# One tile's hat to GpSimd and one tile's distances to VectorE in bump attention, with a new order of all engines' work

## The chip, the core and the metric

The kernel runs on one core of a Trainium2 chip, in one launch. The metric is the device time in microseconds. Its engines are TensorE (matrix products), VectorE, ScalarE and GpSimd (elementwise work), and SyncE, which only issues transfers here. Each takes its instructions in the order in which they were written for it, and waits at each for the semaphores that it names. The kernel before takes 1412.91 us, the median of three runs (1410.71 to 1414.18).

## The reference

A decoder of two layers with post-norm, for 4 batches of 512 tokens of width 128, 16 heads of 8. In each batch: a relative-position self-attention, a cross attention on 77 context tokens, a routed feed-forward block (F0), bump attention (BU), a second cross attention, and a block of self-attention and mixture of experts, twice. A layer norm follows each.

The change is in bump attention. Each head has a key coordinate and a query coordinate for every token, and a bandwidth b; a value counts with a hat function of the distance of the coordinates:

```python
# out_i = sum_j max(0, 1 - |z_i - z_j|/b_h) * v_j, via prefix sums + searchsorted
bw = jax.nn.softplus(log_bw.astype(jnp.float32)) + BW_EPS
...
q_proj = q.reshape(B, T, H * D) @ Wproj.T
k_proj = k.reshape(B, T, H * D) @ Wproj.T
...
ctx = jnp.take_along_axis(ctx_sorted, inv_idx[..., None], axis=2)[:, :, T:]
ctx = ctx / jnp.asarray(T, ctx.dtype)
```

The kernel doesn't sort. It computes for every head the whole 512 x 512 matrix of min(|z_k - z_q|, b) - b, which is the hat times -b, and multiplies it with the values; the factor is put right at the end (column 5 of `bw`).

## The kernel before

Two lanes each own half of the on-chip memory and four of the eight PSUM banks. Lane 0 takes batches 0 and 2, lane 1 batches 1 and 3. A lane goes through stages: A (first self-attention), then for each batch X0 (cross attention), F0, BU, X1 (second cross attention), S0 and M0 (self-attention, experts), S1 and M1. For every stage and engine a generator function issues that engine's instructions and yields at fixed points. `weave` merges the two lanes' generators by a string of bits, `ORDER`, one for each engine: each bit says which lane goes on to its next yield. These strings are written into the file as numbers. So the order of the two lanes' work on an engine is fixed in advance.

Bump attention, in one lane, for each of 16 heads h:

- TensorE, `spread(h)`, L1232: writes the head's query coordinates to all 128 partitions of a PSUM bank, 512 columns. Two banks take turns.
- ScalarE, `bump_scalar`, L1291: four activations, one for each tile kb of 128 keys: absolute value of the bank plus the tile's negated key coordinates (`zk`, one number a partition), into `dist`, 128 x 4 x 512 float32. There are three such buffers in a lane (`L.dist[h % 3]`, parts of `sb_arena`), so head h waits for the product of head h - 3.
- VectorE, `bump_vector`, L1337: one tensor_scalar over all four tiles (2048 columns), minimum with b and then minus b: the hat.
- TensorE, `weighted_values(h)`, L1241: four products, one a tile, with that tile's values, into a bank that collects four heads.

After each four heads ScalarE copies the bank away (`keep`, L1282), and at the end TensorE folds the four row groups of each copy into token rows (L1267), VectorE adds the result to the residual stream (L1341) and normalises it, with GpSimd taking the root (L458, L459). Before the heads GpSimd fills two buffers with zeros (L1303, L1304), VectorE makes the coordinates (L1312, L1320 to L1324) and the values (L1328).

Around it stand F0, in which VectorE picks the expert's weights of a batch by a row of dependent operations (L1192, L1194, L1200, L1202), and X1, whose query parts are cut into three bfloat16 parts by VectorE (L474 to L481) and stacked through memory by SyncE's transfers, whose masks GpSimd makes (L1048 to L1050), and whose first products are L913 and L917. On GpSimd the norm's instructions of one lane stand between the other work of both.

## Time and profile before

| | |
|---|---|
| median of the runs | 1412.91 us |
| the profiled execution | 1408.09 us, span 1406.4 us |
| mean granted clock of TensorE | 0.871 of full speed |
| busy: TensorE | 1182.3 us, 84% of the span |
| VectorE | 758.4 us, 54% |
| ScalarE | 672.0 us, 48% |
| GpSimd | 344.1 us, 24% |
| L1291, the distances, 256 activations | 153.1 us busy |
| L1337, the hats, 64 operations | 89.3 us busy, 39.8 us idle just before them, for L1291 |

The span is the time from the first to the last instruction of one execution that the hardware profiler recorded; the rest of the time lies around it. Busy shares are means over stages with quite different limits: the two bump attentions of the two pairs of lanes take less than 200 us of the span together. What an instruction waited for is told by the semaphore that released it. A duration in the trace includes the time in which an instruction is held up after it has begun; where instructions of an engine overlap, the sum of their durations is more than the busy time.

### The profile page before, as it was taken

Reading aid. Unit: us, or ns where it says so; the run is one execution under the profiler, and the core shown is the slowest. Engines: PE = TensorE matmul, PEld = TensorE weight load, DVE = VectorE, ACT = ScalarE, POOL = GpSimd, SP = SyncE. Lnnn points to the kernel's source line nnn. Section 1 sums busy time; section 2 is a strip of 40 time slices with the busy share of each in tenths; the row PEclk is TensorE's granted clock in tenths of the full one; section 3 lists DMA queues with packets and bytes.
Section 4 is the critical chain, followed back from the end, with each engine's and each line's share of the span. In section 5 each row is a group of like instructions: output and inputs, shape, how many; then the busy total and the mean of one; then the engine's idle time right before and its main releaser. Section 6 shows DMA issues by size and latency. Waiting matters only on the chain.

```text
span 1406.4 us, 20670 instructions
## 1 busy us (share of the span) xinstructions
PE 1182.3 (84%) x7705; PEld 693.5 (49%) x7766; DVE 758.4 (54%) x1977; ACT 672.0 (48%) x1164; POOL 344.1 (24%) x735
## 2 busy tenths in 40 slices
PE   7849767888789999969987877778869999978986
PEld 5735421344344667734565441244434467754455
DVE  2834586574594321278345577557487331159343
ACT  1115369724238643316743538934317753324751
POOL 3121120341235200034403121043324400032510
PEclk8778667877699999999999968878679999999988
DMA  7031000120330000060014100021150000042011
GB/s 240 2 77 41 10 0 1 51 56 7 99 91 3 5 1 1 1 180 3 3 61 106 28 10 1 2 64 43 48 141 3 4 2 1 0 131 51 3 38 38
DMA packets 48354, 57.92 MB, mean 41 GB/s; under 512 B 16469, under 2 KB 41349, under 8 KB 47750
## 3 DMA queue, kind: packets, MB, share of 16 engines
q1 hardware_dynamic: 47390, 56.11, 15.0%
q8 instruction: 62, 1.02, 0.3%
q10 hardware_dynamic: 864, 0.48, 0.1%
q14 instruction: 38, 0.31, 0.1%
HBM read 35.11 MB, written 20.87 MB: 40 GB/s over the span
## 4 chain that ended last, share of the span: by engine, by line
PE 62%; DVE 17%; ACT 9%; POOL 4%; DMA 3%; issue 3%; SPq 1%; another core or an unknown queue 0%; ACTq 0%; POOLq 0%; DVEq 0%
PE banks L1607 10%; PE banks L1597 9%; ACT sb_arena L1291 5%; PE banks L1414 5%; PE banks L1402 4%; PE banks L597 4%; PE banks L1389 3%; PE banks L468 3%; DVE sb_rmax L1542 3%; PE banks L949 2%; PE banks L463 2%; DMA sb_qs<-sb_mrows 2%; DVE sb_arena L1337 1%; DVE sb_st L440 1%; PE banks L913 1%
## 5 line engine op out<-in xcount | busy, mean ns | idle before, releaser
L1542 DVE TENSOR_REDUCE sb_rmax<-banks 128x1 f32<-128x512 f32 (+3 forms) x352 | 204.4, 635 | 67.0 <-PE banks L1391 66.4
L1471 ACT ACTIVATE sb_arena<-banks 128x512 f32<-128x512 f32 x320 | 175.2, 598 | 99.3 <-PE banks L1402 90.1
L1291 ACT ACTIVATE sb_arena<-banks,sb_zk 128x512 f32<-128x512 f32 x256 | 153.1, 800 | 9.3 <-PE banks L1241 9.3
L458 POOL TENSOR_SCALAR sb_var<-sb_mv 128x4 f32<-128x4 f32 x40 | 13.3, 333 | 587.3 <-DVE sb_mv L443 587.3
L1662 ACT ACTIVATE sb_arena<-banks,sb_b 128x512 f32<-128x512 f32 x128 | 87.5, 687 | 132.8 <-PE banks L1597 131.5
L1500 POOL TENSOR_SCALAR_AFFINE_SELECT sb_arena<-sb_arena 128x256 f32<-128x256 f32 x256 | 99.0, 409 | 177.6 <-ACT sb_arena L1471 177.2
L1389 PE MATMUL banks<-sb_arena,sb_qs 128*128 128x256 bf16 (+3 forms) x492 | 119.6, 313 | 26.5 <-DVE sb_rmax L1542 19.9
L1607 PEld LDWEIGHTS banks<-sb_w,sb_arena 128*128 128x128 f32 x1024 | 124.9, 192 | 30.5 <-issue 29.7
L1721 DVE SCALAR_TENSOR_TENSOR sb_xall<-banks,sb_region,sb_xall 128x128 f32<-128x128 f32 x160 | 44.9, 344 | 162.6 <-PE banks L1607 162.6
L1607 PE MATMUL banks<-sb_w,sb_arena 128*128 128x128 f32 x1024 | 126.2, 275 | 0.0
L1597 PE MATMUL banks<-sb_ft,sb_w 128*128 128x512 f32 x256 | 123.7, 597 | 0.6 <-ACT sb_arena L1662 0.6
L1337 DVE TENSOR_SCALAR sb_arena<-sb_arena,sb_bw 128x2048 f32<-128x2048 f32 x64 | 89.3, 1406 | 39.8 <-ACT sb_arena L1291 39.8
L1402 PE MATMUL banks<-sb_qs,sb_arena 128*128 128x256 bf16 (+3 forms) x492 | 102.4, 299 | 9.4 <-DMA sb_qs<-sb_mrows 3.7
L1025 ACT ACTIVATE sb_arena<-banks 77x512 f32<-77x512 f32 x128 | 72.8, 588 | 73.4 <-PE banks L938 55.3
L1241 PE MATMUL banks<-sb_arena 128*32 128x512 f32 x512 | 82.9, 727 | 19.2 <-DVE sb_arena L1337 19.1
L1391 PE MATMUL banks<-sb_trib,sb_identb 128*128 128x128 bf16 (+2 forms) x352 | 89.4, 254 | 4.4 <-DVE sb_rmax L1542 2.3
L1414 PE MATMUL banks<-sb_arena,sb_values 128*32 128x384 f32 (+3 forms) x1024 | 87.3, 441 | 3.9 <-ACT sb_region L1477 2.5
L1389 PEld LDWEIGHTS banks<-sb_arena,sb_qs 128*128 128x128 bf16 x512 | 45.8, 101 | 90.8 <-DVE sb_rmax L1542 47.6
L597 PEld LDWEIGHTS banks<-sb_gather,sb_region 128*128 128x128 f32 x512 | 74.2, 218 | 22.9 <-issue 21.5
L1096 DVE TENSOR_REDUCE sb_rmax<-banks 128x4 f32<-128x308 f32 x128 | 58.1, 473 | 42.8 <-PE banks L917 41.8
L597 PE MATMUL banks<-sb_gather,sb_region 128*128 128x36 f32 x512 | 77.0, 299 | 0.3 <-issue 0.2
L562 ACT ACTIVATE sb_mrows<-banks 12x512 bf16<-12x512 f32 x64 | 36.7, 577 | 70.6 <-PE banks L550 70.4
(281 smaller groups left out, 1936.6 us busy)
## 6 DMA issues: line engine op xcount, KB each, us to landing
sb_qs<-q_scratch SPq DMA_DIRECT2D x32, 288.0 KB, 4.7
q_scratch<-sb_region SPq DMA_DIRECT2D x16, 384.0 KB, 2.6
sb_arena<-k_scratch SPq DMA_DIRECT2D x16, 288.0 KB, 6.8
sb_arena<-in_chosen SPq DMA_DIRECT2D x8, 514.0 KB, 4.1
sb_w<-in_w SPq DMA_DIRECT2D x2, 2048.0 KB
q_scratch<-sb_region SPq DMA_DIRECT2D x16, 256.0 KB, 2.2
sb_qs<-q_scratch SPq DMA_DIRECT2D x32, 96.0 KB, 2.4
k_scratch<-sb_region SPq DMA_DIRECT2D x8, 384.0 KB, 2.6
```

Source lines behind the costliest of these rows:

```text
L597: i = nc.tensor.matmul(ring[pair][:, at:at + GROUP * OW], L.osb[:, g, t * 128:(t + 1) * 128], gather[:].rearrange("p j c -> p (j c)"), sta ...
L1291: i = nc.scalar.activation(L.dist[h % 3][:, kb, :], (b2_, b3)[h % 2], ACT.Abs, bias=L.zk[:, kb, h:h + 1])
L1337: nc.vector.tensor_scalar(L.dist[h % 3], L.dist[h % 3], bw[:, 1, h:h + 1], bw[:, 1, h:h + 1], ALU.min, ALU.subtract).then_inc(L.sem("hat"), 1)
L1389: nc.tensor.matmul(o[:, i * kl:(i + 1) * kl], L.qs[:, h // 2, t * 128:kl], L.ks[:, key_of(h), 0:kl], start=(i == 0), stop=False)
L1391: nc.tensor.matmul(o[:, 0:nh * kl].rearrange("p (h k) -> p h k", k=kl)[:, :, t * 128:kl], identb[:], trib[:].unsqueeze(1).to_broadcast([12 ...
L1402: i = nc.tensor.matmul(o[:, at:at + S - kb * 128], L.ks[:, key_of(h), kb * 128:(kb + 1) * 128], L.qs[:, h // 2, kb * 128:S], start=(n == 0 ...
L1414: last = nc.tensor.matmul(acc[VW * j:VW * (j + 1), kb * 128:S], values_of(L.values[:, kb, :], g * GROUP + j), L.probs[:, (NK * g + n) % SL ...
L1471: nc.scalar.activation(L.probs[:, u % SLOTS, :], bank_of(SELF_ORDER, ring, ("key", u)), ACT.Exp)\
L1500: i = nc.gpsimd.affine_select(out=o, in_=o, pattern=[[0, 2], [1, 128]], compare_op=ALU.is_ge, fill=0.0, base=0, channel_multiplier=-1)
L1542: nc.vector.tensor_reduce(L.rmax[:, t, g * GROUP + h0:g * GROUP + h0 + nh], bank_of(SELF_ORDER, ring, ("max", step))[:, 0:nh * kl] .rearra ...
L1597: nc.tensor.matmul(ups[k % 2], (L.chosen if l else w1)[:, e, at:at + 128], L.ft[:], start=True, stop=True).then_inc(L.sem("up"), 1)
L1607: i = nc.tensor.matmul(downs[o % 2][:, t * 128:(t + 1) * 128], L.hb[:, e % 2, c, t * 128:(t + 1) * 128], second, start=(c == 0), stop=(c = ...
```

## The change

A head's four tiles are split between engines. ScalarE makes the distances of tiles 0 to 2 only. The distances of tile 3 are made by VectorE: `last_distance(h)` adds the key coordinates to the bank (L1349 of the changed kernel), and a bitwise AND with 0x7FFFFFFF clears the sign (L1358). VectorE's hat covers tiles 1 to 3, 1536 columns (L1366). The hat of tile 0 is computed by GpSimd (L1312), which starts after ScalarE's first activation of the head. The wait for the bank and for the free buffer moves from ScalarE to VectorE's `last_distance`, and ScalarE waits for that operation (semaphore `raw`). The product waits for VectorE's hat and GpSimd's (`cut`).

```diff
             def spread(h):
                 if h >= 2:
-                    pe.wait_ge(*p.at("dist", h - 1))
+                    pe.wait_ge(*p.at("dist", 2 * (h - 1)))
...
+                pe.wait_ge(*p.at("cut", h + 1))
                 pe.wait_ge(*p.at("hat", h + 1))
...
             for h in range(H):
                 yield
-                act.wait_ge(*p.at("spread", h + 1))
-                if h >= 3:
-                    act.wait_ge(*p.at("pv", h - 2))
-                for kb in range(T):
+
+                act.wait_ge(*p.at("raw", 2 * h + 1))
+                for kb in range(T - 1):
                     i = nc.scalar.activation(L.dist[h % 3][:, kb, :], (b2_, b3)[h % 2], ACT.Abs,
                                              bias=L.zk[:, kb, h:h + 1])
+                    if kb == 0:
+                        i.then_inc(L.sem("dist"), 1)
                 i.then_inc(L.sem("dist"), 1)
...
             nc.gpsimd.memset(L.bumps, 0.0).then_inc(L.sem("filled"), 1)
+            for h in range(H):
+                yield
+                o = L.dist[h % 3][:, 0, :]
+                pool.wait_ge(*p.at("dist", 2 * h + 1))
+                nc.gpsimd.tensor_scalar(o, o, bw[:, 1, h:h + 1], bw[:, 1, h:h + 1], ALU.min, ALU.subtract)\
+                    .then_inc(L.sem("cut"), 1)
             yield from norm_pool(pool, L, p)
...
+            def last_distance(h):
+
+                dve.wait_ge(*p.at("spread", h + 1))
+                if h >= 3:
+                    dve.wait_ge(*p.at("pv", h - 2))
+                nc.vector.tensor_scalar(L.dist[h % 3][:, T - 1, :], (b2_, b3)[h % 2], L.zk[:, T - 1, h:h + 1], None,
+                                        ALU.add).then_inc(L.sem("raw"), 1)
+
+            yield
+            last_distance(0)
             for h in range(H):
                 yield
-                dve.wait_ge(*p.at("dist", h + 1))
-                nc.vector.tensor_scalar(L.dist[h % 3], L.dist[h % 3], bw[:, 1, h:h + 1], bw[:, 1, h:h + 1],
-                                        ALU.min, ALU.subtract).then_inc(L.sem("hat"), 1)
+                dve.wait_ge(*p.at("raw", 2 * h + 1))
+                o = L.dist[h % 3][:, T - 1, :].bitcast(I32)
+                nc.vector.tensor_scalar(o, o, 0x7FFFFFFF, None, ALU.bitwise_and).then_inc(L.sem("raw"), 1)
+                if h + 1 < H:
+                    yield
+                    last_distance(h + 1)
+                yield
+                dve.wait_ge(*p.at("dist", 2 * h + 2))
+                dve.wait_ge(*p.at("raw", 2 * h + 2))
+                o = L.dist[h % 3][:, 1:T, :]
+                nc.vector.tensor_scalar(o, o, bw[:, 1, h:h + 1], bw[:, 1, h:h + 1], ALU.min, ALU.subtract)\
+                    .then_inc(L.sem("hat"), 1)
```

The strings of `ORDER` are new on all five engines; one line of them:

```diff
     "SP":
-    "3055d943e00ff901fe69a03f9598019fd0fe007fe01fe53a03f95998",
+    "2f531667008dfa01fe53a03f9598037f4d1e08cfe01fe53a03f95998",
```

What they do, at three places. First VectorE where the first pair's heads begin, before the change. A name's last digit is the lane; `x7` is a run of like instructions.

```order
L1187 TENSOR_SCALAR sb_region1<-sb_region1 128x8 [waits dve_chain]
L1337 TENSOR_SCALAR sb_arena0<-sb_arena0,sb_bw 128x2048 [waits l0_dist]
L1190 TENSOR_TENSOR sb_region1<-sb_bdown,sb_region1 64x8
L1191 TENSOR_REDUCE sb_bds1<-sb_region1 64x1 [waits dve_chain]
L1192 TENSOR_SCALAR sb_region1<-sb_wdown,sb_region1 128x64 [waits dve_chain]
L1194 SCALAR_TENSOR_TENSOR sb_region1<-sb_wdown,sb_region1 128x64 [waits dve_chain] x7
L1337 TENSOR_SCALAR sb_arena0<-sb_arena0,sb_bw 128x2048 [waits l0_dist]
L1200 TENSOR_SCALAR sb_region1<-sb_wup,sb_region1 65x128
L1202 SCALAR_TENSOR_TENSOR sb_region1<-sb_wup,sb_region1 65x128 [waits dve_chain] x7
```

Lane 0's hats stand between the steps of lane 1's F0. In the changed kernel the two lanes' F0 alternate (L1193 to L1209), and the first head of either lane comes only after both are normalised; the rows where the heads begin:

```order
L1321 SCALAR_TENSOR_TENSOR sb_zk0<-banks,sb_zkbias 128x64 [waits l0_k]
L1329 CAST sb_k32_0<-sb_q32_0 16x512 [waits l0_filled,l0_q32]
L1330 TENSOR_TENSOR sb_nrm0<-sb_q32_0,sb_k32_0 16x512 [waits dve_chain]
L1331 CAST sb_k32_0<-sb_nrm0 16x512 [waits dve_chain]
L1332 CAST sb_k32_0<-sb_nrm0 16x512 [waits dve_chain]
L1333 TENSOR_TENSOR sb_k32_0<-sb_nrm0,sb_k32_0 16x512
L1349 TENSOR_SCALAR sb_arena1<-banks,sb_zk1 128x512 [waits l1_spread]
L1337 TENSOR_TENSOR sb_arena0<-banks,sb_rows 128x16x8 [waits l0_v]
```

Lane 1's first distances (L1349) now stand right beside lane 0's preparation: the lanes run their heads in step. Further on, in the middle of the heads, VectorE's rows repeat in threes, the add for the next head of one lane, the AND of the other, and the hat:

```order
L1366 TENSOR_SCALAR sb_arena1<-sb_arena1,sb_bw 128x1536 [waits l1_raw,l1_dist]
L1349 TENSOR_SCALAR sb_arena0<-banks,sb_zk0 128x512 [waits l0_pv,l0_spread]
L1358 TENSOR_SCALAR sb_arena1<-sb_arena1 128x512 [waits l1_raw]
L1366 TENSOR_SCALAR sb_arena0<-sb_arena0,sb_bw 128x1536 [waits l0_raw,l0_dist]
L1349 TENSOR_SCALAR sb_arena1<-banks,sb_zk1 128x512 [waits l1_pv,l1_spread]
```

The add for a head stands ahead of the hat of the head before it in the same lane. On GpSimd the first pair's bump attention reads before the change:

```order
L1303 MEMSET sb_k32_0 96x512 [waits l0_ln]
L1304 MEMSET sb_arena0 128x2048
L458 TENSOR_SCALAR sb_var1<-sb_mv1 128x4 [waits l1_stats]
L459 TENSOR_TENSOR sb_rstd1<-sb_var1,sb_half 128x4 [waits pool_chain]
L1166 MEMSET sb_x5_1 128x512 [waits l1_ln]
```

and in the changed kernel, where the hats of both lanes, 32 in all (L1312), follow without other work between them:

```order
L1306 MEMSET sb_k32_0 96x512 [waits l0_ln]
L1307 MEMSET sb_arena0 128x2048
L1312 TENSOR_SCALAR sb_arena1<-sb_arena1,sb_bw 128x512 [waits l1_dist] x2
L1312 TENSOR_SCALAR sb_arena0<-sb_arena0,sb_bw 128x512 [waits l0_dist] x2
L1312 TENSOR_SCALAR sb_arena1<-sb_arena1,sb_bw 128x512 [waits l1_dist]
```

Neither lane's next norm comes before the last of these 32.

## Rows read from the trace of the kernel before

**Rows 1.** The page, part 4: lines of the chain, share of the span.

```profile
PE banks L1607 10%; PE banks L1597 9%; ACT sb_arena L1291 5%; PE banks L1414 5%; PE banks L1402 4%; PE banks L597 4%; PE banks L1389 3%; PE banks L468 3%; DVE sb_rmax L1542 3%; PE banks L949 2%; PE banks L463 2%; DMA sb_qs<-sb_mrows 2%; DVE sb_arena L1337 1%; DVE sb_st L440 1%; PE banks L913 1%
```

**Rows 2.** Timeline, ScalarE and VectorE: start us, us, what, [idle before <-releaser].

```profile
219.18 13.44 ACT L1291 ACTIVATE sb_arena<-banks,sb_zk 128x512 f32<-128x512 f32 x23
...
221.66 1.35 DVE L1337 TENSOR_SCALAR sb_arena<-sb_arena,sb_bw 128x2048 f32<-128x2048 f32 x1 [1.25 <-ACT sb_arena L1291]
223.97 1.35 DVE L1337 TENSOR_SCALAR sb_arena<-sb_arena,sb_bw 128x2048 f32<-128x2048 f32 x1 [0.97 <-ACT sb_arena L1291]
```

**Rows 3.** Windows: length, busy of five engines, clock, DMA, GB/s; last row L1337 alone.

```profile
core 0: us, PE busy (x) PEld busy (x) DVE busy (x) ACT busy (x) POOL busy (x), PEclk, DMA share, GB/s
146.20:186.30 40.10, 29.99 (x141) 17.60 (x142) 26.47 (x109) 11.49 (x24) 10.14 (x14) 0.67 0.03 9
186.30:207.50 21.20, 12.05 (x60) 3.28 (x59) 18.14 (x51) 18.95 (x35) 2.27 (x2) 0.81 0.00 0
219.20:256.00 36.80, 28.63 (x165) 7.66 (x165) 20.26 (x16) 36.80 (x66) 0.00 (x0) 0.81 0.00 1
...
283.90:365.00 81.10, 70.77 (x381) 34.94 (x385) 49.82 (x125) 30.23 (x54) 26.56 (x50) 0.69 0.12 30
...
186.30:207.50 21.20, 7.93 (x6) 0.81 0.00 0
```

**Rows 4.** The chain of waits in order of time: start us, us, what.

```profile
193.59 1.26 DVE sb_arena L1337
```

**Rows 5.** Timeline, ScalarE and VectorE, first and last of the first pair's heads.

```profile
186.27 4.15 ACT L1291 ACTIVATE sb_arena<-banks,sb_zk 128x512 f32<-128x512 f32 x7
...
272.82 1.41 DVE L1337 TENSOR_SCALAR sb_arena<-sb_arena,sb_bw 128x2048 f32<-128x2048 f32 x1
```

**Rows 6.** VectorE: two groups by form (busy us, mean ns), then its timeline.

```profile
L1117 DVE SCALAR_TENSOR_TENSOR banks<-banks,sb_maskt 77x512 f32<-77x512 f32 x64 | 43.0, 689 | 21.0 <-PE banks L931 14.9 <-remote 5.9
...
L1730 DVE COPY sb_k<-banks 8x512 f32<-8x512 f32 x8 | 5.4, 670 | 0.0
...
182.03 0.42 DVE L1323 CAST sb_k<-sb_nrm 16x512 bf16<-16x512 f32 x1
182.46 0.68 DVE L1324 TENSOR_TENSOR sb_k<-sb_nrm,sb_k 16x512 bf16<-16x512 f32 x1
...
217.81 2.59 DVE L1337 TENSOR_SCALAR sb_arena<-sb_arena,sb_bw 128x2048 f32<-128x2048 f32 x2
```

**Rows 7.** GpSimd's groups by form: busy us, mean ns, idle before.

```profile
L1048 POOL TENSOR_SCALAR sb_cbias<-sb_mask 128x308 bf16<-128x308 int32 x4 | 7.0, 1745 | 0.3
...
L1484 POOL COPY sb_x<-sb_xall 128x512 f32<-128x512 f32 x4 | 2.4, 611 | 5.8 <-DVE sb_xall L449 5.8
```

**Rows 8.** L458's durations (ns min/median/max), then timeline, VectorE beside GpSimd.

```profile
L458 POOL TENSOR_SCALAR sb_var<-sb_mv x40: 226/230/1231, 148.3 to 1401.1; 128x4 f32<-128x4 f32 x40
...
203.91 1.32 DVE L1337 TENSOR_SCALAR sb_arena<-sb_arena,sb_bw 128x2048 f32<-128x2048 f32 x1
204.08 1.23 POOL L458 TENSOR_SCALAR sb_var<-sb_mv 128x4 f32<-128x4 f32 x1 [21.59 <-DVE sb_mv L443]
...
207.50 4.63 DVE L1337 TENSOR_SCALAR sb_arena<-sb_arena,sb_bw 128x2048 f32<-128x2048 f32 x2
...
294.81 1.42 DVE L478 CAST sb_region<-sb_region 128x512 bf16<-128x512 f32 x1
```

**Rows 9.** Timeline, TensorE, the last products of lane 1's cross attention X0.

```profile
158.70 3.91 PE L597 MATMUL banks<-sb_gather,sb_region 128*128 128x36 f32 x24
```

**Rows 10.** Timeline after the heads, TensorE and VectorE; then the page, part 6.

```profile
276.15 7.04 PE L1267 MATMUL banks<-sb_fold,sb_region 128*128 128x32 f32 x32
283.00 0.45 PE L913 MATMUL banks<-sb_cbias,sb_identb 128*128 128x308 bf16 x1
...
296.75 0.67 DVE L481 TENSOR_TENSOR sb_region<-sb_region 128x512 bf16<-128x512 f32 x1
...
q_scratch<-sb_region SPq DMA_DIRECT2D x16, 256.0 KB, 2.2
sb_qs<-q_scratch SPq DMA_DIRECT2D x32, 96.0 KB, 2.4
```

37 lines of the change are left out of this document (19 added, 18 removed).

## Prediction

> **What bounds the kernel now.** I read the chain of waits first. Most of its lines are TensorE's; the one large line of ScalarE is L1291, the distances of bump attention, with 5% of the span, some 70 us [rows 1]. So the stage that is changed is the one stretch that ScalarE sets, and outside it the change can only move the order.
>
> Next the timeline of the first bump attention of each lane (batches 0 and 1; the second pair, at 838 to 930 us, is built alike). Where both lanes run heads, ScalarE never rests: 23 activations in 13.44 us, 0.58 us each, so four of them, one head, take 2.31 us. The VectorE operation of each head starts 2.31 us after the last one, takes 1.35 us and waits 0.97 us for ScalarE [rows 2]. ScalarE is busy 36.8 of 36.8 us there, VectorE 20.3 [rows 3].
>
> Before that, from 186 to 207 us, it is another picture. Lane 0 runs heads alone while lane 1 is still in its routed feed-forward stage F0, and VectorE is busy 18.1 of 21.2 us, only 7.9 of them with its six operations for heads [rows 3], and one of these, which F0's next step had to wait for, stands in the chain of waits [rows 4]. So some 6 to 9 (21.2 / 2.31) of the 32 heads are hidden beside F0 of the other lane, because heads cost VectorE little and ScalarE much. The heads start at 186.3 and their last VectorE operation ends at 274.2 us [rows 5].
>
> **The change part by part, for one pair of lanes.** Times are of the profiled execution, 1408.1 us (span 1406.4), which is 4.8 us under the median of the runs, 1412.9; I add that at the end.
>
> ScalarE: four activations a head become three, 1.73 us in place of 2.31. It gives up 32 x 0.58 = 18.5 us a pair and stops being the bound; the eight copies of sums (L1282) are hidden from then on.
>
> VectorE: one operation a head becomes three. (1) The add of the distance, 512 elements out of PSUM: not in the trace; a copy of 512 out of PSUM takes 0.67 us, and L1117, which reads a bank, 0.69; one after another takes some 0.1 less than a duration (below) [rows 6]. I take 0.60 (bounds 0.55 and 0.70). (2) The bitwise AND, 512 elements in SBUF: a cast of 512 starts its successor 0.43 us later, and the two-input operation L1324 on 512 takes 0.68, the slower rate [rows 6]. I take 0.44; upper end 0.60. (3) The hat over 1536 instead of 2048: from 2048 in 1.35 and 512 in 0.44 comes 0.59 us per 1000 elements and 1.04 us; two of the long ones in a row take 2.59, so a pitch is 0.10 less than a duration, 0.95. Sum 1.99 us against 1.25 to 1.35: VectorE is the new bound of the heads, at 2.0 us, if nothing disturbs it. That leaves 0.3 of the 0.58 us that ScalarE saves.
>
> GpSimd: one tensor_scalar of 512 float32, two operations. No such form is in the trace. Lower bound 0.61 us, a copy of 512; from above, the two-operation tensor_scalar on 308 int32 takes 1.75 us, which scaled to 512 is 2.8 [rows 7]. The copy is float32 to float32 with one input, as this one is; the other converts and compares. So I stand near the copy: 0.75 us. The Trainium skill (GPSIMD Engine Reference, Engine selection) says that one-input elementwise work there runs at roughly line rate; with the 1.2 GHz of that page's specifications and 0.23 us fixed that is an estimate of 0.66 us, and the sum below would be 3 us a pair less. The rows of integer tensor_scalar are slower than that rule.
>
> Then the two engines meet. While VectorE ran a hat that started at 203.91 us, a GpSimd tensor_scalar of 4 columns (0.23 us where nothing runs) took 1.23 us and ended 0.08 us after the hat. The other way round, two hats issued when GpSimd's memsets of the bump stage were took 4.63 us, not 2.59, and a cast of 512 took 1.42 [rows 6, 8]. So each keeps the other out for whole instructions. Before the change the steady stretch holds no GpSimd instruction at all [rows 3]; now it holds one a head. The Trainium skill (SBUF — State Buffer, Who interferes with whom) has the rule: the shared port pair is an exclusive lock, taken by a VectorE operation in a two-port mode and by any GpSimd operation, for the whole instruction. By that rule only the PSUM add may run beside GpSimd, and these three rows agree; without it GpSimd would cost nothing here.
>
> From the rows: the GpSimd operation becomes free to run while the hat of the other lane holds VectorE, starts behind it, lies beside the PSUM add (0.60 us) and holds up the AND for the rest. A head then takes 0.44 + 0.95 + max(0.60, P) + some 0.1 for the handing over, P being GpSimd's time: 2.25 us at P = 0.75, 2.1 at 0.61, 4.3 at 2.8. Against ScalarE's old 2.31 this is next to nothing.
>
> The order: lane 1 and lane 0 now go through F0 together and begin their heads together, and GpSimd's 32 operations stand in one row ahead of both lanes' next norms. What VectorE has to do outside the heads from 146 us, when lane 0 left cross attention, until both lanes are prepared is 26.5 us to 186.3, 18.1 - 7.9 = 10.2 more to 207.5, and some 4 (seven operations of 0.2 to 0.9) to prepare lane 1: some 41 us [rows 3]. In the new order the first lane leaves cross attention later, near 159 us: TensorE's last sums of lane 1 ran to 162.6, lane 0 now shares them, and a few us of F0 are out of the way [rows 9]. 159 + 41 = 200 us, and only then do the 32 heads begin, all of them at VectorE's pace. First head 2.5 us (its add, three activations), 32 x 2.25 = 72: the last hat ends at 274.5, where it ended at 274.2.
>
> After the heads both lanes need the fold (7.0 us of TensorE for a lane), norm, projections and splits; lane 1 took 23.2 us from its last hat (274.2) to its last split before cross attention X1 (297.4), and some 4.6 more for the two transfers (2.2 and 2.4), 302 [rows 5, 10]. Lane 0 had this behind it and began X1 at 283.0, as soon as TensorE was done with lane 1's fold [rows 10]. Mean of the two lanes: 292.5. Now both have it at the end: lane 1 took 27.8 us in all, less some 5.8 for the part of the fold that the first lane has earlier, so 274.5 + 22 = 296.5 for the first and 2 to 3 later for the second, mean 297.5 to 298. That is 5 us later a pair. X1 then is a TensorE stretch (70.8 of 81.1 us busy, at a granted clock of 0.69 [rows 3]), which can't win it back. Two pairs: +10 us. 1408.1 + 10 + 4.8 = 1423 us.
>
> **The rivals.**
> A, faster. GpSimd's operation is as short as the copy and fits under the add, the heads go at 2.0 us, and F0 of both lanes packs 4 us better: last hat at 196 + 2.5 + 64 = 262.5, X1 at a mean of 285.5, 7 us a pair, 14 in all: 1399 us. For it: VectorE sits idle 13.6 us in 40 from 146 to 186, which two lanes in step could fill [rows 3]. Against it: the blocked instructions of [rows 8].
> B, clearly slower: GpSimd's float tensor_scalar costs like the integer ones. It decides from P = 1.1 us. At P = 1.3 a head is 2.8 us, the last hat 17.5 us later, both pairs +45: 1458; at 2.8 us (4.3 a head) over 1540.
> C, no change: the heads at 2.1 us, 5 us a pair earlier than I say, which is just what the lost overlap costs: 1413.
> D, the change doesn't relieve ScalarE: an activation now waits for VectorE's add of its head, so a late add stalls it. In the order the add of head h+1 stands ahead of the hat of head h, so this needs VectorE to be the bound, which is counted above. The order of the self-attention and expert stages is nearly as it was; I leave 5 us either way for it.
>
> **How the numbers follow.** Forecast (a head at 2.15 to 2.6 us) 0.45, A 0.27, B 0.17, C 0.11. The forecast's own range is 1412 to 1445. The range that leaves out 2 in 10 reaches from A, 1400, to B at P = 1.3, 1460. What a measurement can tell from no change is 0.3%, 4.2 us. Slower: nearly all of the forecast and B, 0.61; faster 0.27; the same 0.12.
>
> **What would show it.** In the profile after: activations of the heads at 3 x 0.58 us with idle time between, released by VectorE; VectorE near 90% busy through the heads, with the three operations at 0.67, 0.44 and 1.04 us, the latter two longer where GpSimd runs; GpSimd's at 0.75 us alone and up to 1.8 us where it waits behind a hat; heads of the first pair from about 200 to 275 us. Wrong if a head takes under 2.05 us (A), if GpSimd's operation alone is over 1.1 us (B), or if both lanes start their heads before 195 us.

## The result, and the profile after

The changed kernel takes 1475.34 us (median of four runs, 1473.67 to 1487.6) against 1413.55 us for the kernel before in the same session: ratio 1.045, 95% interval 1.038 to 1.052. The forecast was 1423 us, the range 1400 to 1460. The direction was right, the size was not: 62 us slower instead of 10. Some executions of a kernel fall into a slower state; the medians here are over all its runs, the ratios leave those executions out, so a ratio need not be the quotient of two medians.

The page of the changed kernel, lines of part 1 (busy us, share, instructions), part 4 (the chain) and part 5 (groups: count, busy us, mean ns, idle before):

```profile
PE 1227.8 (83%) x7766; PEld 715.0 (49%) x7766; DVE 815.5 (55%) x2105; ACT 639.4 (43%) x1100; POOL 495.6 (34%) x799
...
PE 61%; DVE 18%; POOL 12%; ACT 3%; DMA 2%; issue 2%; SPq 1%; ACTq 0%; POOLq 0%; DVEq 0%
PE banks L1636 9%; POOL sb_arena L1312 9%; PE banks L1626 9%; PE banks L1443 5%; DVE sb_rmax L1571 5%; PE banks L598 5%; PE banks L1431 4%; PE banks L950 3%; PE banks L469 3%; PE banks L1418 2%; PE banks L668 2%; PE banks L1243 2%; PE banks L464 2%; PE banks L939 2%; PE banks L1269 1%
...
L1312 POOL TENSOR_SCALAR sb_arena<-sb_arena,sb_bw 128x512 f32<-128x512 f32 x64 | 163.3, 2563 | 23.0 <-ACT sb_arena L1292 23.0
...
L1292 ACT ACTIVATE sb_arena<-banks,sb_zk 128x512 f32<-128x512 f32 x192 | 115.6, 696 | 42.6 <-DVE sb_arena L1349 42.3
...
L1243 PE MATMUL banks<-sb_arena 128*32 128x512 f32 x512 | 94.0, 824 | 45.4 <-POOL sb_arena L1312 39.2
...
L1366 DVE TENSOR_SCALAR sb_arena<-sb_arena,sb_bw 128x1536 f32<-128x1536 f32 x64 | 80.3, 1272 | 1.2 <-ACT sb_arena L1292 1.2
```

Where the chain of before had ScalarE's distances with 5% [rows 1], it has GpSimd's hat of tile 0 with 9%. ScalarE is relieved: it waits 42.3 us for VectorE's add, as forecast. But TensorE's product now waits 39.2 us for GpSimd, and VectorE isn't the bound. The reason is the mean of L1312: 2563 ns, against 750 assumed.

The timeline, GpSimd, VectorE and ScalarE in the middle of the first pair's heads, and the first pair's last hats:

```profile
220.75 16.83 POOL L1312 TENSOR_SCALAR sb_arena<-sb_arena,sb_bw 128x512 f32<-128x512 f32 x7
...
226.16 1.36 DVE L1366 TENSOR_SCALAR sb_arena<-sb_arena,sb_bw 128x1536 f32<-128x1536 f32 x1
227.45 0.74 DVE L1349 TENSOR_SCALAR sb_arena<-banks,sb_zk 128x512 f32<-128x512 f32 x1
228.11 0.43 DVE L1358 TENSOR_SCALAR sb_arena<-sb_arena 128x512 int32<-128x512 int32 x1
228.24 1.86 ACT L1292 ACTIVATE sb_arena<-banks,sb_zk 128x512 f32<-128x512 f32 x3
228.46 1.36 DVE L1366 TENSOR_SCALAR sb_arena<-sb_arena,sb_bw 128x1536 f32<-128x1536 f32 x1
...
274.36 0.75 DVE L1349 TENSOR_SCALAR sb_arena<-banks,sb_zk 128x512 f32<-128x512 f32 x1 [5.77 <-PE banks L1243]
275.02 1.07 DVE L1366 TENSOR_SCALAR sb_arena<-sb_arena,sb_bw 128x1536 f32<-128x1536 f32 x1
275.93 2.63 POOL L1312 TENSOR_SCALAR sb_arena<-sb_arena,sb_bw 128x512 f32<-128x512 f32 x1 [1.31 <-ACT sb_arena L1292]
```

GpSimd runs seven hats in 16.83 us without a gap, 2.40 us each, where ScalarE needed 2.31 us a head [rows 2]. VectorE's hat is 1.36 us beside it and 1.07 us where it is free, so it is slowed by a quarter, not shut out. The chain of waits says the same of the bound: from 232.4 to 262.8 us it holds nothing but GpSimd's hats, twelve in 30.4 us.

What became of the stretch of hats (first VectorE hat to end of the last), the changed kernel, then the kernel before; columns as in [rows 3]:

```profile
197.80:278.10 80.30, 56.55 (x292) 10.76 (x291) 69.67 (x93) 59.50 (x100) 78.99 (x32) 0.73 0.00 1
882.50:968.20 85.70, 61.11 (x293) 13.95 (x293) 73.18 (x93) 59.11 (x100) 80.44 (x32) 0.70 0.00 1
```

```profile
189.50:274.20 84.70, 62.53 (x351) 17.31 (x351) 61.45 (x95) 78.57 (x137) 12.38 (x11) 0.84 0.01 3
837.70:927.50 89.80, 62.72 (x351) 17.50 (x351) 63.34 (x97) 78.58 (x137) 17.34 (x14) 0.84 0.05 15
```

GpSimd is busy for 79 of 80 us in the first pair and for 80 of 86 in the second. Before, the stretch was longer but held part of F0 and of X1 of the other lane as well; after, it holds heads alone, and TensorE's granted clock in it is 0.73 and 0.70 instead of 0.84.

The four ends of cross attention from X0 of the second pair on (L1125 before, L1126 after), the kernel before and then the changed kernel:

```profile
792.30 0.69 DVE L1125 TENSOR_TENSOR sb_xall<-banks,sb_xall 128x512 f32<-128x512 f32 x1 [0.78 <-PE banks L468]
822.12 0.69 DVE L1125 TENSOR_TENSOR sb_xall<-banks,sb_xall 128x512 f32<-128x512 f32 x1 [2.43 <-PE banks L468]
993.31 0.69 DVE L1125 TENSOR_TENSOR sb_xall<-banks,sb_nrm 128x512 f32<-128x512 f32 x1 [0.98 <-PE banks L468]
1020.73 0.69 DVE L1125 TENSOR_TENSOR sb_xall<-banks,sb_nrm 128x512 f32<-128x512 f32 x1 [2.45 <-PE banks L468]
```

```profile
825.80 0.69 DVE L1126 TENSOR_TENSOR sb_xall<-banks,sb_xall 128x512 f32<-128x512 f32 x1 [5.25 <-PE banks L469]
835.98 0.69 DVE L1126 TENSOR_TENSOR sb_xall<-banks,sb_xall 128x512 f32<-128x512 f32 x1 [1.20 <-PE banks L469]
1065.27 0.69 DVE L1126 TENSOR_TENSOR sb_xall<-banks,sb_nrm 128x512 f32<-128x512 f32 x1 [1.01 <-PE banks L469]
1091.31 0.69 DVE L1126 TENSOR_TENSOR sb_xall<-banks,sb_nrm 128x512 f32<-128x512 f32 x1 [3.54 <-PE banks L469]
```

Taking the mean of the two lanes, X0 of the second pair ends at 807.2 before and 830.9 after, X1 at 1007.0 and 1078.3. So the first pair costs 24 us, and the second, from X0's end to X1's, 47 more (199.8 against 247.4). The forecast had the two pairs cost alike; they don't. These are single executions. Another one of the same work, e5 below up to its tail, ends X0 at a mean of 819.4 us and takes 201.9 to X1's end, and the changed kernel again (e15) has 830.6 and 246.6: the 24 of the first pair are uncertain by some 12 us, the 47 of the second by some 2.

### The profile page after: what moved, and what is told of

It reads as the page before. It is cut to its first block, busy times and chain, and to the rows that moved or that the text cites. A ratio compares the mean times of both kernels' runs of the same rounds, so it can differ in the third digit from the quotient of the medians.

```text
span 1473.4 us, 20977 instructions
## 1 busy us (share of the span) xinstructions
PE 1227.8 (83%) x7766; PEld 715.0 (49%) x7766; DVE 815.5 (55%) x2105; ACT 639.4 (43%) x1100; POOL 495.6 (34%) x799
## 4 chain that ended last, share of the span: by engine, by line
PE 61%; DVE 18%; POOL 12%; ACT 3%; DMA 2%; issue 2%; SPq 1%; ACTq 0%; POOLq 0%; DVEq 0%
PE banks L1636 9%; POOL sb_arena L1312 9%; PE banks L1626 9%; PE banks L1443 5%; DVE sb_rmax L1571 5%; PE banks L598 5%; PE banks L1431 4%; PE banks L950 3%; PE banks L469 3%; PE banks L1418 2%; PE banks L668 2%; PE banks L1243 2%; PE banks L464 2%; PE banks L939 2%; PE banks L1269 1%
## 5 line engine op out<-in xcount | busy, mean ns | idle before, releaser
L1571 DVE TENSOR_REDUCE sb_rmax<-banks 128x1 f32<-128x384 f32 (+3 forms) x352 | 204.6, 634 | 70.8 <-PE banks L1420 70.2
L1312 POOL TENSOR_SCALAR sb_arena<-sb_arena,sb_bw 128x512 f32<-128x512 f32 x64 | 163.3, 2563 | 23.0 <-ACT sb_arena L1292 23.0
L1418 PE MATMUL banks<-sb_arena,sb_qs 128*128 128x128 bf16 (+3 forms) x512 | 128.7, 320 | 21.4 <-DVE sb_rmax L1571 14.4
L1292 ACT ACTIVATE sb_arena<-banks,sb_zk 128x512 f32<-128x512 f32 x192 | 115.6, 696 | 42.6 <-DVE sb_arena L1349 42.3
L1243 PE MATMUL banks<-sb_arena 128*32 128x512 f32 x512 | 94.0, 824 | 45.4 <-POOL sb_arena L1312 39.2
L1431 PE MATMUL banks<-sb_qs,sb_arena 128*128 128x512 bf16 (+3 forms) x512 | 108.0, 302 | 7.4 <-ACT sb_mrows L563 2.3
L598 PEld LDWEIGHTS banks<-sb_gather,sb_region 128*128 128x128 f32 x512 | 84.4, 239 | 32.4 <-issue 24.9
L1443 PE MATMUL banks<-sb_arena,sb_values 128*32 128x256 f32 (+3 forms) x1024 | 86.6, 440 | 2.7 <-ACT sb_region L1506 2.7
L598 PE MATMUL banks<-sb_gather,sb_region 128*128 128x36 f32 x512 | 86.9, 317 | 0.0
L1366 DVE TENSOR_SCALAR sb_arena<-sb_arena,sb_bw 128x1536 f32<-128x1536 f32 x64 | 80.3, 1272 | 1.2 <-ACT sb_arena L1292 1.2
```

Of the source, the lines that this page charges most:

```text
L598: i = nc.tensor.matmul(ring[pair][:, at:at + GROUP * OW], L.osb[:, g, t * 128:(t + 1) * 128], gather[:].rearrange("p j c -> p (j c)"), sta ...
L1243: i = nc.tensor.matmul((b0, b1_)[g % 2][kb * VW:(kb + 1) * VW, :], L.bumps[:, kb, h, :], L.dist[h % 3][:, kb, :], start=(h % GROUP == 0), ...
L1292: i = nc.scalar.activation(L.dist[h % 3][:, kb, :], (b2_, b3)[h % 2], ACT.Abs, bias=L.zk[:, kb, h:h + 1])
L1312: nc.gpsimd.tensor_scalar(o, o, bw[:, 1, h:h + 1], bw[:, 1, h:h + 1], ALU.min, ALU.subtract)\
L1418: nc.tensor.matmul(o[:, i * kl:(i + 1) * kl], L.qs[:, h // 2, t * 128:kl], L.ks[:, key_of(h), 0:kl], start=(i == 0), stop=False)
L1431: i = nc.tensor.matmul(o[:, at:at + S - kb * 128], L.ks[:, key_of(h), kb * 128:(kb + 1) * 128], L.qs[:, h // 2, kb * 128:S], start=(n == 0 ...
```

## The experiments

Theory PRICE: GpSimd's operation itself is dear and sets the pace. Theory ORDER: what costs is that no head lies beside F0 or X1 of the other lane. Theory LOCK: VectorE and GpSimd shut each other out for whole instructions. All ratios are to the kernel before, run on the same chip between them.

### e1: GpSimd's hat on 4 columns

The other 508 columns of tile 0 keep their distances and never become a hat.

```diff
-                nc.gpsimd.tensor_scalar(o, o, ...
+                nc.gpsimd.tensor_scalar(o[:, 0:4], o[:, 0:4], ...
```

> The changed kernel, but GpSimd's hat covers 4 of its 512 columns; the other 508 columns of tile 0 are left out of the hat. Theory PRICE: what makes the changed kernel slower is the GpSimd operation, 2.1 us alone and 2.4 us beside VectorE, which bounds the heads at 2.4 to 2.5 us. Without it VectorE bounds them at 2.0 to 2.1 us, 32 x 0.4 = 13 us a pair, and with what follows from it the time comes back to 1413 or less. Theory ORDER: the price is a part only; what costs is that no head runs beside F0 or X1 of the other lane any more. Then only the 13 us a pair come back, 1475 - 26 = 1445 to 1450, with the X1 of both lanes still starting together after the last head. Theory LOCK: VectorE's hat stays at 1.07 us here, against a median of 1.36 in the changed kernel.

Measured: 1418.49 us, ratio 0.998 (0.995 to 1.001). All of the loss is gone, not half of it. Its windows of hats, and two of its groups:

```profile
198.90:261.70 62.80, 47.16 (x300) 10.76 (x300) 61.28 (x93) 58.37 (x100) 27.35 (x31) 0.93 0.00 1
853.50:916.80 63.30, 48.19 (x308) 11.79 (x307) 61.47 (x94) 58.52 (x100) 36.24 (x31) 0.92 0.00 1
...
L1366 DVE TENSOR_SCALAR sb_arena<-sb_arena,sb_bw 128x1536 f32<-128x1536 f32 x64 | 67.3, 1069 | 2.1 <-ACT sb_arena L1292 2.1
L1312 POOL TENSOR_SCALAR sb_arena<-sb_arena,sb_bw 128x4 f32<-128x4 f32 x64 | 64.7, 1014 | 77.4 <-ACT sb_arena L1292 77.3
```

VectorE is busy 61.3 of 62.8 us: 31 heads after the first in 61.7 us are 1.99 us each, the sum of the prediction. GpSimd's 4 columns, 0.23 us in [rows 8], take 1.01 us here: it is held up behind VectorE's hats, which lose nothing (1069 ns). And the clock in the hats is 0.93.

### e2: the work of before in the new order

```diff
-                for kb in range(T - 1):
+                for kb in range(T):        # ScalarE; no add, no AND, no GpSimd hat
```

> The work of the kernel before (ScalarE four activations a head, VectorE the hat over 2048 columns, GpSimd nothing) in the order of the changed kernel. PRICE: near the kernel before, 1405 to 1425, since GpSimd's operation is gone. ORDER: heads at 2.31 us, ScalarE bound, beginning at about 196 us and ending at 272 to 275, so some 3 to 5 us a pair better than the changed kernel, 1465, and over 1450 in any case, because neither F0 nor X1 has heads beside it.

Measured: 1448.44 us, ratio 1.011 (1.000 to 1.022). Hats from 196.9 to 274.0 and from 864.3 to 941.0. The four ends of X0 and X1 are at 811.93, 819.34, 1032.83 and 1058.87. The first pair's mean, 815.6, lies between two executions of the work of before (807.2 and 819.4), so no cost is shown there; the second pair takes 230.2 us instead of 199.8. So ORDER holds for a part, and that part is in the second pair.

Some 17 of these 30 us are X1's, measured against the first pair's X1. From its first product to its last end it took 75.0 us at a granted clock of 0.77 after the first pair's hats, and 92.1 us at 0.59 after the second's, with the same work. e1 has the same two values (73.9 at 0.77, 92.1 at 0.59). e9 below, in the same order, has not (71.9 at 0.80, 78.8 at 0.75). Why the clock is so low there in most kernels of the new order was not tested.

### e3: the split in the old order; e4: a half split in the old order

In e3 the split stays, in the order of before; add, AND and hat share one place. In e4, on top of before, only odd heads have tile 3 made by VectorE, and GpSimd has nothing.

```diff
+                if h % 2:
+                    dve.wait_ge(*p.at("raw", h // 2 + 1))
+                    ... the AND of tile 3 of head h
+                else:
+                    ... the add of tile 3 of head h + 1, which waits for spread and pv
                 dve.wait_ge(*p.at("dist", h + 1))
```

> The split of the changed kernel (three activations, the add, the AND, a hat over 1536 columns, GpSimd's hat of tile 0) in the order of the kernel before; on GpSimd, where the kernel before has no hats, each hat stands where VectorE's stands in time. PRICE: GpSimd still bounds the heads at 2.4 us or more, 1460 or over. ORDER: heads at 2.4 instead of 2.31, 32 x 0.1 to 0.2 = 3 to 6 us a pair, 1420 to 1430.

> The kernel before in its own order, and only of every second head (the odd ones) tile 3's distances are made by VectorE, add and AND; nothing goes to GpSimd, the hat stays one operation of 2048 columns. A head then costs ScalarE 3.5 x 0.58 = 2.02 us in place of 2.31 and VectorE 1.25 + (0.64 + 0.44) / 2 = 1.8 us. If ScalarE's work is what bounds the heads, each saves 0.29 us where both lanes run heads, some 20 to 32 heads a pair, 6 to 9 us a pair: 1395 to 1402. If the order is made for ScalarE's pace and VectorE's place in it is the limit (its add stands in a slot behind a hat of the other lane), no change, 1410 to 1418.

Measured: e3 1473.58 us, ratio 1.034 (1.028 to 1.040), hats 106 and 113 us long; e4 1432.31, 1.011 (1.006 to 1.015), hats 97 and 94 us. e4's gain did not come. In the old order a head's add stands behind the other lane's hat, and that waits for ScalarE, which waits for an add. In e4, where GpSimd has nothing, ScalarE waits 36.9 us for adds; in e3 it is 85.3 us, against 42.3 in the changed kernel. Two of e3's waits, GpSimd and ScalarE:

```profile
223.77 7.04 POOL L1312 TENSOR_SCALAR sb_arena<-sb_arena,sb_bw 128x512 f32<-128x512 f32 x3
...
224.65 1.84 ACT L1292 ACTIVATE sb_arena<-banks,sb_zk 128x512 f32<-128x512 f32 x3 [5.10 <-DVE sb_arena L1349]
...
233.72 1.84 ACT L1292 ACTIVATE sb_arena<-banks,sb_zk 128x512 f32<-128x512 f32 x3 [4.79 <-DVE sb_arena L1349]
```

ScalarE stands some 5 us before one add. The first of the two goes back to GpSimd: the add waited 4.0 us for the product of an earlier head, and that 4.9 us for GpSimd's hat. The second add stood behind VectorE's preparation of the other lane (L1321 to L1337, 227.9 to 232.7 us). Later in e3 GpSimd runs eight hats in 18.92 us without a gap. So e3's time is what PRICE expected, but late adds and GpSimd's price are mixed in it, and it doesn't tell them apart. Late adds alone, the prediction's rival D, are e4: the same work in the new order, with a place of its own for each operation, is e9 below, with hats of 68 and 70 us instead of 97 and 94 (the kernel before: 85 and 90). A form in which VectorE adds behind ScalarE wasn't tried.

### e5: forms of GpSimd by themselves

A tail after the last stage of before, with one engine alone, then both.

```diff
+                ts(d0[:, 0, :], 3)        # minimum, subtract; also 256 and 64 columns
+                ... minimum alone; multiply, add with constants; minimum, subtract with constants;
+                ... add alone; tensor_tensor add; copy; then 8 and 6 ts and 12 copies beside VectorE
```

> The kernel before with a tail after its last stage, in which GpSimd alone, then VectorE alone, then both beside each other run single forms on dead data. PRICE: GpSimd's min and subtract on 128x512 takes 2.07 us with nothing beside it, and so it is the operation and not the lock; half the columns take about half. What makes it dear is either two operations (then one operation alone takes about 1.1 and multiply and add on 512 also 2.1), or minimum (then multiply and add takes about 0.7, min alone 2.0), or the scalar read from memory (then the same with constants takes less). LOCK: with VectorE's hats of 1536 beside it, GpSimd's takes 2.1 to 2.6 us and the hat 1.35 us in place of 1.07; with VectorE's adds out of PSUM beside it neither grows. If each kept the other out for whole instructions, a hat would be over 2 us beside it.

GpSimd's groups by form in the tail: L1812 is minimum and subtract with b from memory (its 512-column row mixes alone and beside VectorE), L1818 minimum, L1820 multiply and add with constants, L1822 minimum and subtract with constants, L1824 add of b, L1826 tensor_tensor add, L1828 copy:

```profile
L1822 POOL TENSOR_SCALAR sb_arena<-sb_arena 128x512 f32<-128x512 f32 x2 | 3.8, 1920 | 0.2
L1824 POOL TENSOR_SCALAR sb_arena<-sb_arena,sb_bw 128x512 f32<-128x512 f32 x2 | 3.2, 1577 | 0.2
L1818 POOL TENSOR_SCALAR sb_arena<-sb_arena,sb_bw 128x512 f32<-128x512 f32 x2 | 3.1, 1556 | 0.2
L1826 POOL TENSOR_TENSOR sb_arena<-sb_arena 128x512 f32<-128x512 f32 x2 | 2.5, 1259 | 0.2
L1812 POOL TENSOR_SCALAR sb_arena<-sb_arena,sb_bw 128x256 f32<-128x256 f32 x2 | 2.4, 1214 | 0.2
L1820 POOL TENSOR_SCALAR sb_arena<-sb_arena 128x512 f32<-128x512 f32 x2 | 1.2, 618 | 0.2
L1828 POOL COPY sb_arena<-sb_arena 128x512 f32<-128x512 f32 x2 | 1.2, 610 | 0.1
```

Then the phases beside VectorE, GpSimd's and VectorE's groups: first hats of 1536 (L1858) beside L1812, then L1812 beside adds out of PSUM (L1862, not shown), then hats beside copies (L1840):

```profile
L1812 POOL TENSOR_SCALAR sb_arena<-sb_arena,sb_bw 128x512 f32<-128x512 f32 x8 | 20.2, 2524 | 6.6 <-DVE sb_arena L1873 5.9
L1858 DVE TENSOR_SCALAR sb_arena<-sb_arena,sb_bw 128x1536 f32<-128x1536 f32 x12 | 15.9, 1321 | 0.4
...
L1812 POOL TENSOR_SCALAR sb_arena<-sb_arena,sb_bw 128x512 f32<-128x512 f32 x6 | 12.4, 2067 | 0.8 <-DVE sb_arena L1876 0.3
...
L1840 POOL COPY sb_arena<-sb_arena 128x512 f32<-128x512 f32 x8 | 10.0, 1246 | 0.7 <-DVE sb_arena L1879 0.3
L1858 DVE TENSOR_SCALAR sb_arena<-sb_arena,sb_bw 128x1536 f32<-128x1536 f32 x8 | 9.8, 1225 | 0.3
```

The hat costs GpSimd 2.07 us alone (three, mean 2071 ns) and with adds beside it, the same as the shortest one in the changed kernel (2061 ns); it is the operation. Neither of the guesses of a single cause holds: multiply and add with constants is as fast as the copy, 0.62 us, so two operations are not dear as such; minimum with constants is slow (1.92), and so is one add with b read from memory (1.58). The assumed price was that of another form.

Beside hats, GpSimd goes from 2.07 to 2.52 us and the hat from 1.08 (three alone, 3.31 us with their waits) to 1.32. Twelve hats (13 us alone) and some six GpSimd operations (12.4 us) fit into 15.9 us. If each held the other out for whole instructions it would be 25 us.

### e10: a cheap form in the same place

```diff
-                nc.gpsimd.tensor_scalar(o, o, bw[:, 1, h:h + 1], bw[:, 1, h:h + 1], ALU.min, ALU.subtract)\
+                nc.gpsimd.tensor_scalar(o, o, 1.0, 0.5, ALU.mult, ALU.add)\
```

> The changed kernel, but GpSimd's operation on the 512 columns of tile 0 is multiply and add with constants, the form that took 0.62 us alone, in place of minimum and subtract; the hat of tile 0 is left out. It is what the prediction had assumed of GpSimd (0.75 us). By the sum of the prediction (lock for whole instructions) a head is 2.1 to 2.25 us, hats of a pair 68 to 72 us, and the time 1425 to 1440 by what kernels with such hats took. If the lock holds only for parts of an instruction, as the 1.25 us of a hat beside copies says, GpSimd hides and a head is 2.0 to 2.1 us: 63 to 67 us, 1418 to 1425.

Measured: 1428.49 us, ratio 1.006 (1.002 to 1.011); hats 65.5 and 69.3 us long, clock 0.88 and 0.85, GpSimd 0.96 us a piece, VectorE's hat 1131 ns. With the price that the prediction assumed, the kernel is where the prediction had it: 1.0062 x 1413.55 = 1422 us. Only the total agrees: the heads take 2.08 and 2.20 us instead of 2.25, and the second pair 218 us from X0's end to X1's against 200, where 5 more were forecast.

### e7, e8, e9, e17: between the two

e7: GpSimd takes 256 columns, VectorE 1792. e8: VectorE makes the hat of all 2048 columns, GpSimd nothing. e9: in the new order, tile 3 by VectorE for odd heads only, hat of 2048, GpSimd nothing. e17: GpSimd's minimum alone.

```diff
-                o = L.dist[h % 3][:, 0, :]
+                o = L.dist[h % 3][:, 0, 0:256]                                          # e7
-                o = L.dist[h % 3][:, 1:T, :]
+                o = L.dist[h % 3].rearrange("p t n -> p (t n)")[:, 256:2048]            # e7
+                o = L.dist[h % 3]                                                       # e8
-                for kb in range(T - 1):
+                for kb in range(T - h % 2):                                             # e9
-                nc.gpsimd.tensor_scalar(o, o, b, b, ALU.min, ALU.subtract)
+                nc.gpsimd.tensor_scalar(o, o, b, None, ALU.min)                         # e17
```

> The changed kernel, but GpSimd does the hat of 256 columns of tile 0 and VectorE that of the other 1792 of the head's 2048. PRICE: GpSimd 1.1 to 1.3 us, no longer the bound; VectorE 0.64 + 0.41 + 1.15 to 1.35 = 2.2 to 2.4 us a head, the hats of a pair last 70 to 75 us (80 and 86 in the changed kernel, 63 with the small operation): 1430 to 1445. LOCK for whole instructions would give 0.41 + 1.2 + 1.2 + 0.1 = 2.9 us a head, more than the changed kernel.

> The changed kernel without any GpSimd hat: VectorE makes tile 3's distances and the hat of all four tiles in one operation. VectorE is the bound with 0.64 + 0.41 + 1.25 = 2.3 us a head, hats of a pair 73 to 75 us. PRICE: 1435 to 1445, 30 us better than the changed kernel though VectorE has more to do. If what costs is the dependence of ScalarE on VectorE's add, it stays at 1460 or more.

> The order of the changed kernel, in which add, AND and hat have places of their own; VectorE makes tile 3's distances for every second head only, the hat is one operation of 2048 columns, GpSimd has nothing. ScalarE 2.02 us a head, VectorE 1.8. If places were what made every-second slow in the old order (hats 97 and 94 us), the hats now last 65 to 67 us and the time is that of the small operation, 1415 to 1425; if it is the dependence itself, the hats stay over 80 us.

> The changed kernel with GpSimd's minimum alone, without the subtraction (1.56 us alone, against 2.06); the subtraction of tile 0 is left out. PRICE: GpSimd takes 1.56 us and what VectorE holds it up, 0.4 to 0.7 us more, so 2.0 to 2.2 us a head, about VectorE's own pace: hats of a pair 68 to 72 us, 1430 to 1440, the greater part of the loss gone with half a us of GpSimd. If the time follows the operation's cost in proportion (1428 at 0.62, 1475 at 2.07), it is 1459.

All in the new order, by length of the hats (us, first and second pair), with the granted clock in them:

| kernel | GpSimd's operation alone, in the heads | hats | clock | median | ratio |
|---|---|---|---|---|---|
| e1 | 0.23, 1.01 | 62.8, 63.3 | 0.93, 0.92 | 1418.5 | 0.998 |
| e10 | 0.62, 0.96 | 65.5, 69.3 | 0.88, 0.85 | 1428.5 | 1.006 |
| e9 | none | 68.1, 69.6 | 0.87, 0.89 | 1420.6 | 1.004 |
| e7 | 1.21, 2.17 | 69.5, 70.2 | 0.84, 0.87 | 1436.9 | 1.011 |
| e8 | none | 71.4, 72.3 | 0.82, 0.83 | 1442.0 | 1.013 |
| e17 | 1.56, 2.32 | 73.9, 79.6 | 0.79, 0.74 | 1449.5 | 1.017 |
| e2 | none | 77.1, 76.7 | 0.80, 0.87 | 1448.4 | 1.011 |
| changed | 2.07, 2.56 | 80.3, 85.7 | 0.73, 0.70 | 1475.3 | 1.045 (e15: 1.031) |

The time goes roughly with the length of the hats, whichever engine sets it; e2, with its wide interval, fits least. e8, with nothing on GpSimd, shows the other side: there VectorE's longer hat sets 2.3 us a head. e7 is decisive for PRICE against LOCK: GpSimd's half is stretched from 1.21 to 2.17 us, yet a head is 2.2 us, VectorE's own sum, and not the 2.9 of whole-instruction locks. GpSimd's operation costs next to nothing until it is longer than what VectorE needs for a head. e17 was expected at 1430 to 1440; its 1449.5 lies between the threshold and the proportional price (1459), because at 2.32 us it is already past VectorE's pace.

### e11, e12, e13, e15, e16: is it the clock?

From e1 to the changed kernel the hats grow by 40 us in all, the span by 55. On the page TensorE's busy time grows from 1183.1 to 1227.8 us, but e1's trace lacks 61 of the 7766 matmuls of the same program, some 20 us by the means of their lines. What is left lies in the heads and just behind them: 21.6 us more in the products of L1243 and 6.7 in the folds (L1269). The same product took, in e1, in the kernel before and in the changed kernel:

```profile
L1243 PE MATMUL banks<-sb_arena 128*32 128x512 f32 x512 | 72.4, 645 | 1.5 <-DVE sb_arena L1366 1.3
```

```profile
L1241 PE MATMUL banks<-sb_arena 128*32 128x512 f32 x512 | 82.9, 727 | 19.2 <-DVE sb_arena L1337 19.1
```

so 645, 727 and, above, 824 ns. That the lower clock is an effect of TensorE's waiting, and can be bought back, was tried by issuing each head's spread product twice: in the changed kernel (e11, e16), before (e12) and in e9 (e13); e15 is the changed kernel again.

```diff
-                nc.tensor.matmul((b2_, b3)[h % 2], ..., start=True, stop=True).then_inc(L.sem("spread"), 1)
+                for _ in range(2):
+                    i = nc.tensor.matmul((b2_, b3)[h % 2], ..., start=True, stop=True)
+                i.then_inc(L.sem("spread"), 1)
```

> The changed kernel, with each head's spread product issued twice (the same values into the same bank), which keeps TensorE busier while GpSimd sets the pace. Theory CLOCK: TensorE's granted clock, 0.83 in the changed kernel against 0.871, is low because TensorE waits in the heads (58 of 82 us busy at 0.73), and it takes some 40 of the 62 us; busier, the clock in the heads rises over 0.8 and the time falls by 10 us or more. Rival: the clock falls with more work, the time rises by 5 to 15 us (64 x 0.4 us of products that are partly in the way). If neither, within 5 us of 1475.

> The kernel before with each head's spread product issued twice. CLOCK: TensorE is 38 of 47 us busy in the heads at 0.84 already; little changes there, 1410 to 1425, lower only if the clock after the heads rises. Rival (more work, less clock): 1425 to 1440.

> The new order with every second head's tile 3 by VectorE and nothing on GpSimd (1420.6 us, the same as before), and the spread twice. CLOCK: over 64 heads TensorE is busier; 1400 to 1415, which would be faster than both kernels. Rival: 1430 or more, since a head of 2.02 us leaves TensorE (1.8 us a head and 0.4 more) no room and it becomes the bound at 2.2 us.

> The changed kernel itself, beside the next two on the same chip: ratio 1.04 to 1.05 as before.

> The changed kernel with the spread product issued twice, now beside the changed kernel. CLOCK: it does more and is still faster, by 8 to 12 us, at a granted clock higher by 0.01. Rival: the difference between 1475 and 1466 was one of sessions, and here the two are within 3 us of each other or the one with more work is slower.

Measured: e11 1465.83 (ratio 1.033, 1.024 to 1.043); e12 1422.69 (1.002, 0.998 to 1.006); e13 1430.08 (1.009, 1.004 to 1.015); side by side, e15 1474.45 (1.031, 1.023 to 1.038) and e16 1469.46 (1.033, 1.028 to 1.038). The clock of whole executions is mostly higher with the second product (0.833 to 0.847 in e16, 0.820 to 0.849 in e15), but the times can't be told apart; by the medians of their six runs e15 is at 1.037 and e16 at 1.034 of the kernel before. In the heads the clock did rise with the second product, from 0.73 and 0.68 (e15) to 0.78 and 0.76 (e16), and the hats lasted as long: 80.1 and 85.8 us, then 79.4 and 84.8. In the new order without GpSimd it is the same (e9 0.87 and 0.89, 68.1 and 69.6 us; e13 0.90 and 0.95, 68.9 and 70.5). So the product is slower at the lower clock, the lower clock goes in part with TensorE's waiting, and it isn't what makes the hats long. What sets the clock in the stages behind them stays open.

### e14, e18, e19: new order for the first pair, old order for the second

e14 takes e9 for the first pair and the kernel before, work and order, for the second; e18 has the same two orders without any split; e19 is e14 again.

```diff
+        self.stages += [(kind, b) for b in range(u, B, LANES)
+                        for kind in [("BV" if k == "BU" and b >= LANES else k) for k in ROUND]]
```

> For the first pair of batches the order of the changed kernel with every second head's tile 3 by VectorE and no GpSimd hat; for the second pair the work and the order of the kernel before. In profiles the first led to the second pair's start at a mean of 800.6 us against 807.2, the second took 200 us from there to the end of X1 against 213. If both add up, 6 us under the kernel before: ratio 0.995. If the order's price in the second pair is only the clock of that one execution, the ratio is 1.000 to 1.005, as for the kernel that used the new order throughout (1.0039).

> The order of the changed kernel for the first pair of batches, that of the kernel before for the second, and the work of the kernel before in both (ScalarE four activations a head, no split). If the gain of e14 (ratio 0.992) is the order of the first pair alone, this is 0.99 to 0.995 too. If it is the every-second split, which ended the first pair's hats at 264 us against 273 with the whole of the distances on ScalarE, this is 1.000 to 1.005.

> The kernel e14 again, beside e18 on the same chip. If its gain is real, the ratio is 0.988 to 0.996 once more; if it was one of that session, it lies within 0.3% of the kernel before.

Measured: e14 1410.41 us, ratio 0.992 (0.988 to 0.996); e19 1413.29, 0.992 (0.988 to 0.996); e18 1419.24, 0.999 (0.996 to 1.003). This version is faster than both kernels, than the kernel before by 0.8%. Its four ends, as above:

```profile
789.25 0.69 DVE L1115 TENSOR_TENSOR sb_xall<-banks,sb_xall 128x512 f32<-128x512 f32 x1 [1.17 <-PE banks L458]
818.31 0.69 DVE L1115 TENSOR_TENSOR sb_xall<-banks,sb_xall 128x512 f32<-128x512 f32 x1 [1.67 <-PE banks L458]
988.61 0.69 DVE L1115 TENSOR_TENSOR sb_xall<-banks,sb_nrm 128x512 f32<-128x512 f32 x1 [1.01 <-PE banks L458]
1017.63 0.69 DVE L1115 TENSOR_TENSOR sb_xall<-banks,sb_nrm 128x512 f32<-128x512 f32 x1 [2.37 <-PE banks L458]
```

The second pair takes 199.3 us again (e9, in the new order throughout, 212.9), 13.5 us less, which is most of the 1.2% between e9 and e14. The first pair gains only with the split: e18 without it is as fast as before, and its first hats last 77.1 us against 68.1.

## Why the prediction was wrong

By its own steps:

- **ScalarE, three activations:** right. They take 1.84 us (forecast 1.73), with idle time released by VectorE's add.
- **VectorE, 1.99 us a head:** right. e1 shows it: 0.74, 0.41 and 1.07 us, which overlap by 0.1 or less at each start, 1.99 us a head. But it never was the bound of the changed kernel.
- **GpSimd, P = 0.75 us: this is the step that failed.** It is 2.07 us alone and 2.56 in the heads. Both bounds stood in the prediction (0.61 from a copy, 2.8 scaled from two-operation integer tensor_scalars [rows 7]), and the value was taken from the wrong one: the copy was nearer in type, the tensor_scalar nearer in operation. The upper bound was too high besides: it scaled a mean of 1.75 us in which some of the four operations of L1048 were held up (1.26 to 2.32 us). The shortest, 1.26, scaled in the same way, gives an estimate of 2.0 us, nearly what came. The rule of the Trainium skill (GPSIMD Engine Reference, Engine selection), one-input work at roughly line rate, agrees with the copy (0.61) and with multiply and add by constants (0.62), and not with this form (2.07). Rival B, "GpSimd clearly slower, from P = 1.1", was the case that came, with a chance of 0.17, and most of it lay outside the range.
- **The lock, a head = 0.44 + 0.95 + max(0.60, P) + 0.1:** wrong as well, and it hid the first mistake's size. With P = 2.07 it gives 3.6 us a head and over 1500 us; measured are 79.2 / 31 = 2.56 and 84.6 / 31 = 2.73. With 1.21 and the longer hat of e7 it gives 2.9, measured 2.2; with 0.62 it gives 2.11, measured 2.08 and 2.2. The rows it was built on were read rightly, but they are of other forms. A short GpSimd instruction does wait behind a hat (e1: 1.01 for 0.23), and the two hats of 4.63 us in [rows 8] waited some 2.0 us beside memsets of 0.52 and 1.80. GpSimd's float32 hat holds up VectorE's for some 0.25 us only, and its copy for 0.15. The Trainium skill (SBUF — State Buffer, Who interferes with whom) states a lock for the whole instruction; the runs agree with it for that short instruction and the memsets, and not for VectorE's hats beside GpSimd's hats and copies.
- **The order:** the first lane left X0 at 146.1 us, not 159, and the hats began at 197.8, near the 200 forecast. That is luck: VectorE had 43.6 us of work up to there (forecast 41) and 8 us of idle time that the sum had not. The last ended at 278.1 (forecast 274.5). X1 then began at 305.9 us (forecast 296.5), where lane 0 had begun at 283.0 [rows 10]. The chain of waits shows what the sum had left out, three masks and an add of a bias row (L1049 to L1052, 5.4 us), which now stand after the 32 hats on GpSimd and ahead of the other lane's key split; behind that split's transfer SyncE issues the one that X1's first product waits for:

```profile
294.40 1.93 POOL sb_maskt L1050
296.33 0.95 POOL sb_mask L1051
297.28 1.23 POOL sb_nrm L1052
...
299.25 0.60 POOL sb_region L490
...
300.79 4.92 DMA sb_qs<-q_scratch
305.85 0.42 PE banks L914
```

The cost was taken as 5 us for each pair; e2, with the heads at ScalarE's old pace, shows none that is clear of the spread in the first and 30 in the second, some 17 of them in X1 at the lower clock.
- **Rivals:** A (faster) was refuted even by e1: heads at 1.99 us, ending at 261.7 us as A said, bring the kernel back to before and no further. In the first pair A's 7 us came (X1 ends at a mean of 350.3 us, before at 358.1), but the second pair of the new order gives them away (219.7 us in e1 against 199.8), with its X1 at 92.1 us where the first pair's took 73.9. C and D are not what happened, though e3 and e4 show D where the order allows it.

The right sum: GpSimd sets a head, 2.07 and some 0.45 of hold-up, 2.5 us, which is 16 us a pair over 1.99; measured are 17.5 and 22.4 (80.3 - 62.8, 85.7 - 63.3). That is 40 of the 55 us between the spans of e1 and the changed kernel. In the second pair TensorE has a part in it: at the end of its hats eight products take 1.87 us, in e1 0.99. The other 15 us are spread: 2 and 7 between the last hat and X1's first product (in the second pair the fold of 32 products alone took 6.97 us against 3.86, at a clock of 0.50 against 0.66 in that stretch), 4 in the first X1, and 7 from there to the second pair's X0 at 0.92 against 0.93, with 5 won elsewhere. They go with a lower granted clock; what lowers it there is not shown.
